# Layer 3 of a four-layer graph network: attention over 440 groups of 512 edges, rewritten with other operands, lead times and buffers

## The reference

```python
h = jnp.maximum(_layernorm(x, axis=-1), 0.0)
# _L3_gnn_ref(h, rel_embed_weight, W, heads=src, rels=edge_type_64, tails=dst)
e_h = entity_emb[heads]
e_t = entity_emb[tails]
e_r = rel_embed_weight[rels]
score = jnp.sum(e_t * jnp.tanh(e_h + e_r), axis=-1)
score_exp = jnp.exp(score - lax.stop_gradient(jnp.max(score)))
score_sum = jax.ops.segment_sum(score_exp, heads, num_segments=n_entities)
attn = score_exp / (score_sum[heads] + 1e-10)
agg = jax.ops.segment_sum(attn[:, None] * e_t, heads, num_segments=n_entities)
out = (entity_emb + agg) @ W.T
return jax.nn.leaky_relu(out, negative_slope=0.2)
```

## Time and profile before

| | us |
|---|---|
| median of 3 runs | 12000.16 |
| lowest, highest run | 11994.03, 12004.05 |
| profiled execution, its own time | 12014.41 |
| its span | 12012.6 |
| PE busy (share of the span) | 8140.2 (68%) |
| PEld busy | 6349.2 (53%) |
| DVE busy | 8287.7 (69%) |
| ACT busy | 4862.3 (40%) |
| POOL busy | 6896.0 (57%) |
| first record load of layer 3 | at 9149.8 |

### The profile page before, as it was taken

One profiled execution on the slowest core, in us unless ns is written; L12 is line 12 of the kernel. 1 busy time (PEld: TensorE's weight loads), 2 busy tenths in 40 slices (PEclk: granted clock), 3 DMA queues, 4 the chain that ended last, 5 costly groups with the idle time before them and its releaser, 6 DMA issues. The chain is left out here.

```text
span 12012.6 us, 257271 instructions
## 1 busy us (share of the span) xinstructions
PE 8140.2 (68%) x63022; PEld 6349.2 (53%) x63685; DVE 8287.7 (69%) x33874; ACT 4862.3 (40%) x9481; POOL 6896.0 (57%) x7087
## 2 busy tenths in 40 slices
PE   0222222255888888867766777777755999999996
PEld 0222222234566555556545666666653777777775
DVE  7444444426888888878526999999987666666664
ACT  3000000003777777722103555555542444444442
POOL 1777777722777777720004777777753666666662
PEclk9999999998888888889857999999987999999997
DMA  3333333330222222146301222222252333333345
GB/s 116 80 80 80 80 80 80 78 29 24 61 60 59 59 58 58 50 121 175 104 11 34 60 59 60 60 59 60 60 46 64 98 99 98 98 99 98 98 97 59
DMA packets 863125, 886.04 MB, mean 74 GB/s; under 512 B 466669, under 2 KB 636430, under 8 KB 862693
## 3 DMA queue, kind: packets, MB, share of 16 engines
q0 software_dynamic: 254464, 511.95, 18.7%
q1 hardware_dynamic: 608613, 373.57, 12.0%
HBM read 699.65 MB, written 155.84 MB: 71 GB/s over the span
## 5 line engine op out<-in xcount | busy, mean ns | idle before, releaser
L1291 POOL DMA_INDIRECT a_far<-node_table,a_rows x3552 | 3464.3, 975 | 3242.7 <-DMA a_rows<-edge_records 1256.1
L1069 POOL DMA_INDIRECT message_records<-f_msg,f_index x1760 | 1746.3, 992 | 924.2 <-issue 528.1
L897 POOL DMA_INDIRECT sum_far<-split_table,sum_rows x1760 | 1669.2, 948 | 669.4 <-issue 631.9
L982 PE MATMUL banks<-sum_far,sum_hot 128*128 128x128 bf16 x5280 | 635.5, 310 | 1711.8 <-DMA sum_far<-split_table,sum_rows 1604.8
L982 PEld LDWEIGHTS banks<-sum_far,sum_hot 128*128 128x128 bf16 x5280 | 528.2, 143 | 1819.0 <-issue 891.1
L964 ACT ACTIVATE acc<-sum_cur 128x128 f32 x880 | 272.2, 309 | 2752.8 <-DVE sum_cur L926 2415.6
L926 DVE SCALAR_TENSOR_TENSOR sum_cur<-sum_cur,gsame,banks 128x128 f32<-128x128 f32 x880 | 303.0, 344 | 1253.6 <-PE banks L982 1250.5
L1429 PE MATMUL banks<-ident,a_score 128*128 128x128 f32 x7072 | 997.1, 287 | 223.2 <-DVE a_score L1351 197.5
L1449 PE MATMUL banks<-a_far,a_prob 128*128 128x129 f32 x7056 | 1029.6, 291 | 0.0
L1429 PEld LDWEIGHTS banks<-ident,a_score 128*128 128x128 f32 x7072 | 994.5, 202 | 32.3
L1393 ACT ACTIVATE a_hot_t<-banks 128x512 bf16<-128x512 bf16 x888 | 521.4, 587 | 1038.6 <-PE banks L1438 749.9
(11 more groups left out here) (271 smaller groups left out, 19179.5 us busy)
## 6 DMA issues: line engine op xcount, KB each, us to landing
a_rows<-message_records SPq DMA_DIRECT2D x446, 264.0 KB
sum_rows<-message_records SPq DMA_DIRECT2D x441, 264.0 KB
acc<-a_cur SPq DMA_DIRECT2D x880, 65.0 KB
a_far<-node_table,a_rows POOLq DMA_INDIRECT x3552
sum_far<-split_table,sum_rows POOLq DMA_INDIRECT x1760
message_records<-f_msg,f_index POOLq DMA_INDIRECT x1760
f_attr<-edge_attributes SPq DMA_DIRECT2D x447, 40.0 KB
edge_attributes<-in_edge_attr SPq DMA_DIRECT2D x8, 1953.1 KB, 33.7
```

The lines of the kernel that those rows point to most:

```text
L897: pool.indirect_dma_start(far[:, u, q, :], None, k.table3[:, :], bass.IndirectOffsetOnAxis(ap=rows[:, u, q, C_SRC:C_SRC + 1].bitcast(I32), ...
L982: last = nc.tensor.matmul(k.psum[a % 2][:, 0:D], hot[:, u, q, :], rhs, start=q == 0 and part == 0, stop=q == KG - 1 and part == (2 if o == ...
L1069: pool.indirect_dma_start(k.mrec[:, :], bass.IndirectOffsetOnAxis(ap=index[:, u, q:q + 1], axis=0), msg[:, u, q, :], None, bounds_check=ED ...
L1291: pool.indirect_dma_start(far[:, u, q, 0:D], None, k.table[:, :], bass.IndirectOffsetOnAxis(ap=rows[:, u, q, other:other + 1].bitcast(I32) ...
```

## The change

Layer 3 no longer calls `attention(k, 1)` but a function of its own, `relation(k)`; layer 2 still uses `attention`. In `relation`:

- The record load takes only the last four words of each edge (512 pieces of 16 bytes a group) into eight buffers, with a lead of 10.
- `columns` (lead 7) makes `rel`, `kind` and `hide`. PE spreads the two as rows over all partitions (`spread_keys`, lead 6: eight bf16 matmuls of a broadcast column with the identity), ACT copies the 128x1024 result as bf16 (`take_keys`), and DVE compares each with the partition's number, which gives the one-hots with edges on the free axis at once (`one_hots`, lead 5: two instructions of 128x512). L1438, L1440, L1392, L1393 and the four-times-two comparisons go.
- The relation's first two parts lie on partitions 0 to 63 and 64 to 127 of one operand, so a block of 128 edges takes two matmuls for it instead of three (`near`, lead 4). The tanh is written back to PSUM, and the score reads it there (lead 3).
- One running maximum over all edges and windows takes the place of one per node. DVE reduces the scores of a partition to one (`peak`), PE spreads the 128 peaks (one f32 matmul), DVE takes their maximum. ACT takes the exponentials of the 128x4 scores only. DVE builds the weighted one-hots in f32 (`weigh`, lead 1: compare and multiply, four instructions of 128x128), with edges on partitions, as PE needs them for the sums. L1427, three of the four f32 matmuls of L1429, L1476, L1386, L1398 and L1359 go.
- The gather has a lead of 6 and eight buffers. `CREDIT` grows to 16 so that no count starts below zero; in layers 1 and 2 it only changes by how much counts are raised at the start.

```diff
--- before.py
+++ after.py
-CREDIT = 10
+CREDIT = 16
 ...
-        rel_f = sb(top, "rel_f", [NTYPE, D])
-        rel3 = sb(top, "rel3", [NTYPE, 3 * D], BF16)
+        rel_f = sb(top, "rel_f", [P, D])
+        rel2 = sb(top, "rel2", [P, 2 * D], BF16)
+        part_id, part_i = sb(top, "part_id", [P, 2]), sb(top, "part_i", [P, 1], I32)
 ...
-                split3(nc, lambda ins: link(dve, ins), rel3[:, 0:D], rel3[:, D:2 * D], rel3[:, 2 * D:3 * D],
-                       rel_f[:, :], relr)
+                split3(nc, lambda ins: link(dve, ins), rel_hi, rel_mid, rel_lo, rel_f[:, :], relr)
+                nc.vector.tensor_copy(rel2[0:NTYPE, 0:D], rel_hi[0:NTYPE, :])
+                nc.vector.tensor_copy(rel2[NTYPE:P, 0:D], rel_mid[NTYPE:P, :])
+                nc.vector.tensor_copy(rel2[0:NTYPE, D:2 * D], rel_lo[0:NTYPE, :])
+                nc.vector.tensor_copy(part_id[:, 0:1], part_i[:, :])
+                link(dve, nc.vector.tensor_scalar(part_i[:, :], part_i[:, :], NTYPE - 1, None, ALU.bitwise_and))
+                link(dve, nc.vector.tensor_copy(part_id[:, 1:2], part_i[:, :]))
 ...
-        attention(k, 1)
+        relation(k)
 ...
+def relation(k):
+    LOAD, COLS, KEYS, GATHER, HOT, NEAR, SCORE, MAX, WEIGH, ADD = 10, 7, 6, 6, 5, 4, 3, 2, 1, 0
+    S, H = 2 * U, 4
 ...
+                def load(g, a):
+                    wait(sp, now, scores, g, a, S)
+                    e0 = first_edge(sp, k, o, g + a)
+                    sp.dma_start(rows[:, a % S, :, :], k.mrec[bass.ds(e0, GE), M_SRC:MW].bitcast(I32).rearrange("(p q) c -> p q c", q=KG))\
+                        .then_inc(loads_in[a % S], 16)
 ...
+                skewed(sp, (LOAD, load), (ADD, keep), counts=now, turn=S)
 ...
+                def gather(g, a):
+                    u = a % S
+                    pool.wait_ge(loads_in[u], slot_count(now, g, a, 16, S, s_load[u]))
+                    wait(pool, now, summed, g, a, S)
+                    pool.sem_inc(k.begun, 1)
+                    for q in range(KG):
+                        pool.indirect_dma_start(
+                            far[:, u, q, 0:D], None, k.table[:, :],
+                            bass.IndirectOffsetOnAxis(ap=rows[:, u, q, M_DST - M_SRC:M_DST - M_SRC + 1], axis=0))\
+                            .then_inc(gathered[u], 16)
+                skewed(pool, (GATHER, gather), counts=now, turn=S)
 ...
+                def columns(g, a):
+                    u = a % S
+                    dve.wait_ge(loads_in[u], slot_count(now, g, a, 16, S, s_load[u]))
+                    nc.vector.tensor_scalar(rel[:, u, :], rows[:, u, :, 0], k.gbase[o][:, bass.ds(g + a, 1)], None, ALU.subtract)
+                    nc.vector.tensor_copy(kind[:, u, :], rows[:, u, :, M_TYPE - M_SRC]).then_inc(cols_ready, 1)
+                    wait(dve, now, cols_ready, g, a)
+                    nc.vector.tensor_scalar(hide[:, u, :], rel[:, u, :], float(P), -BIG, ALU.is_ge, ALU.mult)
+                def one_hots(g, a):
+                    h, b = a % H, a % 2
+                    wait(dve, now, keys_taken, g, a)
+                    wait(dve, now, near_ready, g, a, H)
+                    nc.vector.tensor_scalar(hot_t[:, h, :], keys[:, b, 0, :], k.part_id[:, 0:1], None, ALU.is_equal)
+                    nc.vector.tensor_scalar(kind_t[:, h, :], keys[:, b, 1, :], k.part_id[:, 1:2], None, ALU.is_equal)\
+                        .then_inc(onehotT_ready, 1)
+                def score_edges(g, a):
+                    u, b = a % S, a % 2
+                    dve.wait_ge(gathered[u], slot_count(now, g, a, 16 * KG, S))
+                    wait(dve, now, edge_term, g, a)
+                    wait(dve, now, scores, g, a, 1)
+                    for q in range(KG):
+                        last = nc.vector.scalar_tensor_tensor(
+                            work[:, q, :], near_ps[b][:, q * D:(q + 1) * D], 1.0, far[:, u, q, 0:D], ALU.mult, ALU.mult,
+                            accum_out=raw[:, q:q + 1])
+                    last.then_inc(edge_dot, 1)
+                    wait(dve, now, edge_dot, g, a)
+                    wait(dve, now, weighed, g, a, S)
+                    nc.vector.tensor_tensor(score[:, u, :], raw[:, :], hide[:, u, :], ALU.add).then_inc(masked, 1)
+                    wait(dve, now, masked, g, a)
+                    wait(dve, now, spread, g, a, S)
+                    nc.vector.tensor_reduce(peak[:, u:u + 1], score[:, u, :], AX, ALU.max).then_inc(scores, 1)
+                def running_max(g, a):
+                    u, f = a % S, bass.ds(g + a, 1)
+                    past = cur[:, (u - 1) % S, D + 1:D + 2]
+                    wait(dve, now, exp_in, g, a, 1)
+                    wait(dve, now, shrink, g, a, S)
+                    nc.vector.tensor_scalar(before[:, u:u + 1], past, k.gfresh[o][:, f], None, ALU.add)
+                    wait(dve, now, spread, g, a)
+                    nc.vector.tensor_reduce(gmax[:, :], peak_ps[a % 2][:, 0:P], AX, ALU.max).then_inc(group_max, 1)
+                    dve.wait_ge(kept, now(g, 16 * (a + 1), 16))
+                    wait(dve, now, group_max, g, a)
+                    nc.vector.scalar_tensor_tensor(cur[:, u, D + 1:D + 2], gmax[:, :], -1.0, past, ALU.mult, ALU.min)\
+                        .then_inc(exp_in, 1)
+                def weigh(g, a):
+                    u, b = a % S, a % 2
+                    wait(dve, now, weighed, g, a)
+                    wait(dve, now, summed, g, a, 2)
+                    for q in range(KG):
+                        last = nc.vector.tensor_scalar(share[:, b, q, :], k.iota_b[:, :], rel[:, u, q:q + 1],
+                                                       prob[:, u, q:q + 1], ALU.is_equal, ALU.mult)
+                    last.then_inc(prob_ready, 1)
+                def add(g, a):
+                    u, b = a % S, a % 2
+                    wait(dve, now, summed, g, a)
+                    wait(dve, now, shrink, g, a)
+                    wait(dve, now, added, g, a, 1)
+                    nc.vector.scalar_tensor_tensor(cur[:, u, 0:D + 1], cur[:, (u - 1) % S, 0:D + 1], factor[:, u:u + 1],
+                                                   sum_ps[b][:, 0:D + 1], ALU.mult, ALU.add).then_inc(added, 1)
+                skewed(dve, (HOT, one_hots), (ADD, add), (WEIGH, weigh), (SCORE, score_edges), (MAX, running_max), (COLS, columns),
+                       counts=now, turn=S)
+            @block.scalar
+            def _(act):
+                now = Counts(act)
+                start(act, keys_taken, edge_term, weighed, shrink)
+                def take_keys(g, a):
+                    wait(act, now, keys_spread, g, a)
+                    wait(act, now, onehotT_ready, g, a, 2)
+                    nc.scalar.activation(keys[:, a % 2, :, :], key_ps, ACT.Copy).then_inc(keys_taken, 1)
+                def terms(g, a):
+                    b = a % 2
+                    wait(act, now, near_ready, g, a)
+                    nc.scalar.activation(near_ps[b], near_ps[b], ACT.Tanh).then_inc(edge_term, 1)
+                def exps(g, a):
+                    u = a % S
+                    wait(act, now, exp_in, g, a)
+                    wait(act, now, prob_ready, g, a, S)
+                    nc.scalar.activation(prob[:, u, :], score[:, u, :], ACT.Exp, bias=cur[:, u, D + 1:D + 2]).then_inc(weighed, 1)
+                    wait(act, now, added, g, a, S)
+                    nc.scalar.activation(factor[:, u:u + 1], before[:, u:u + 1], ACT.Exp, scale=-1.0,
+                                         bias=cur[:, u, D + 1:D + 2]).then_inc(shrink, 1)
+                skewed(act, (KEYS, take_keys), (NEAR, terms), (MAX, exps), counts=now, turn=S)
+            @block.tensor
+            def _(pe):
+                now = Counts(pe)
+                start(pe, keys_spread, near_ready, spread, summed)
+                def spread_keys(g, a):
+                    u = a % S
+                    wait(pe, now, cols_ready, g, a)
+                    wait(pe, now, keys_taken, g, a, 1)
+                    for i, col in enumerate((rel, kind)):
+                        for q in range(KG):
+                            last = nc.tensor.matmul(key_ps[:, i, q * P:(q + 1) * P], top_half(col[:, u, q:q + 1]), k.ident_b[:, :],
+                                                    start=True, stop=True)
+                    last.then_inc(keys_spread, 1)
+                def near(g, a):
+                    h, b = a % H, a % 2
+                    w = window(pe, k, o, g + a)
+                    wait(pe, now, onehotT_ready, g, a)
+                    wait(pe, now, scores, g, a, 2)
+                    for q in range(KG):
+                        span = slice(q * P, (q + 1) * P)
+                        for part in range(3):
+                            nc.tensor.matmul(near_ps[b][:, span], hot_t[:, h, span], k.near[:, w, part * D:(part + 1) * D]
+                                             .rearrange("p a d -> p (a d)"), start=part == 0, stop=False)
```

(19 more changed lines are left out.)

69 lines of the change are left out of this document (63 added, 6 removed).

## The result

| | us |
|---|---|
| after, median of 4 runs | 11562.61 (11560.19 to 11566.87) |
| before, median of 4 runs | 11998.98 (11994.03 to 12004.05) |
| ratio | 0.9637, 95% interval 0.962 to 0.9653 |
| profiled execution after, and its span | 11562.07, 11560.3 |

The change makes the kernel 436 us faster. That is the predicted side and inside the range, 42 us above the forecast of 11521 and 3 us above the band of 11486 to 11560 that the prediction gave the forecast itself.

What follows compares the result with a forecast made beforehand. POOL's gathers replace PE as layer 3's limit: 1784 x 1.252 = 2234 us plus 35 for padding, 479 us less in all. The profiled 12014.4 becomes 11535, which lies 14 above the median: 11521, range 11480 to 11720.

Steps and rivals of the forecast that it cites:

- the band of 11486 to 11560: Whole kernel: span of the forecast itself, from the padding's bounds and a few us at the ends; chance 0.66.
- The bound moves from PE to POOL: Layer 3: POOL's four gathers a group, 1.252 us each, set the pace at 5.01 us instead of PE's 6.08.
- the keys: PE in layer 3: the eight matmuls spreading the keys take 0.8 us a group, between 0.76 and 1.44.
- The clock of 0.88: PE in layer 3: at layer 1's granted clock its 3.8 us a group become 4.3.
- The load of the window's number: PE's own queue in layer 3: costed at nothing behind 1.9 us of queued work, up to 1.0 us if late.
- the 0.7 that the prediction promised: Layer 3: DVE would wait some 0.7 us a group for gathers ahead of its products.
- The first rival: Layer 3: DVE or PE ends above POOL; 174 us more, 11695, span 11560 to 11920; chance 0.22.
- 46 ns for each piece: Layer 3's DMA: 1152 pieces at this price take 53 us of the 80 a group has, hidden.
- The rule on the shared port: A two-port tensor_scalar locks GpSimd out of writing descriptors; six such instructions a group would be felt on POOL.
- The rival that built on it: Layer 3: gathers wait for VectorE's comparisons and weighing, 1.3 us a group, 580 us more, 12101; chance 0.04.
- Its sign of being wrong by DMA: Layer 3: POOL's gathers waiting for record loads would show the prediction wrong.
- The padding's term: Layer 3's last 27 groups: 108 gathers at layer 0's 1.57 us each add 35 us, bounds nothing and 68.

Runs made afterwards that it cites:

- Run 3: The changed kernel with PE spreading the peaks four times instead of once a group in layer 3, three more f32 matmuls; 11585.75 us.
- run 1: The changed kernel with layer 3 issuing two of its four gathers a group, output not the reference's; 11437.25 us against 12029.83 for the kernel before.
- run 8: run 1 with 40 groups instead of 8 in a round of layer 3's loops; 11193.85 us against 12010.86 for the kernel before.
- Run 4: The kernel before with only layer 3's narrow record load, four words an edge; 12020.22 us against 12029.83 for the kernel before.
- Run 5: The changed kernel with the padding message records naming different target rows instead of one common row; 11516.44 us, ratio 0.9588.
- run 6: Run 5 with the edge records' padding, loaded by layers 0 to 2, also naming different source rows; 11451.91 us, ratio 0.9536.
- run 10: The changed kernel with 40 groups in a round of layer 3's loops, on a chip where the kernel before took 14715.03 us; 14586.38 us, ratio 0.9905.

## Why the prediction was right, and where it was off

- **The bound moves from PE to POOL**: right. 5.03 us a group against 5.01, gathers 1.25 us apart across groups, and 5.2 us of waiting for `summed` in 1700 us. Run 3 (more PE work, same pace) and run 1 (half the gathers, faster) show it from both sides.
- **PE**: it is hidden, as forecast; its 1472.2 us busy are 4.36 a group, where 4.3 were costed, but partly by luck. At the full clock a turn of PE takes 3.61 us (run 1, 10014.19 to 10017.80) for the 3.8 costed: the keys 0.45 instead of 0.8, the sums 0.99 instead of 0.88. The clock of 0.88 was taken over from layer 1's messages, and the 0.91 measured came from DVE's stall, which the prediction did not have. The load of the window's number was put at nothing; PEld stands some 0.48 us in front of the node rows in nearly every turn (147.1 us in 307 times), which stayed hidden too. Run 3's three more matmuls still found room.
- **DVE**: 4.3 predicted, and a turn that nothing disturbs lasts 4.24 (runs 1 and 8). Within it the weighings are 0.23 dearer (1.03 for 0.8), and products and masking what they were costed at. Missing from the sum was the stall at the end of a loop's round, 3.2 us in eight groups and 5.2 with PE's slower turns behind it: 4.24 + 5.2 / 8 = 4.89, and the next limit is at 4.885 (run 1) instead of 4.3. That is the step that failed. The profile before could not have priced it: in its layer 3, with as many groups in a round, DVE never stands longer than 1.6 us. It stayed hidden, but by 0.15 us and not by the 0.7 that the prediction promised as DVE's wait for gathers; in fact its products waited 47.9 us in the whole stage for them. The first rival was nearer than its chance of 0.22 made it look.
- **DMA**: 46 ns for each piece was wrong for pieces of 16 bytes. Run 4 shows 21 ns as the mean, the share fell from 0.36 to 0.30 although a group is shorter, where 0.5 to 0.65 was forecast. The term was hidden either way.
- **The rule on the shared port** (the Trainium skill, SBUF — State Buffer, "Who interferes with whom"): the trace still speaks against it for these instructions. With two comparisons of 128x512 and four weighings a group the gathers last 954 ns on average (1288.43 / 1351), where layer 0's last 948 (1471.87 / 1553); at most these 6 ns could be the port's. The rival that built on it, 12101 us, is out.
- **Where the 42 us lie.** Start: the first gather at 9146.2, not 9157, because the code before it ran shorter than in the profiled execution before (layer 2's first gather is at 6423.1 already, where it was at 6433.9): -11. Pace: 1672 gathers in 2104 us (to 11250.2) are 1.258 each, not 1.252, by the 6 ns that a gather lasts longer: +11. Padding: the last 112 gathers took 189 us, 1.69 each, where 1.57 was taken over 108 of them: 189 - 112 x 1.252 = 49 instead of 35, +14. End: 16 us from the last gather to the next stage instead of 2: +14. That is +28 against 11535, and the profiled execution was 11562 (+27). The remaining 14 are the offset from the profiled execution to the median: it was a property of that one execution before, and did not come back (11562.07 profiled, 11562.61 median).

Of the signs that the prediction named, POOL's busy share, the distance of the gathers and the 0.35 us of the comparisons came true. Three did not: PE is busy 87% and not 75% to 85%, DVE hardly waits for gathers, and the DMA share is 0.30. Its sign of being wrong by DMA, gathers that wait for record loads, is there in the padding only, 34.0 us.

The padding's term was taken from layer 0 rather than from layer 3's own 1.88: the truth lies between. Run 5 names its cause, one common row, which the prediction used and did not look into; run 6 shows that it is worth more than a quarter of what the change itself gives (121 of 436 us).

## What to carry to other kernels

When one engine is relieved, cost the others with everything that comes with them: here the 0.30 us in front of each gather, and the 3 us that DVE stands at the end of a loop's round, which short rounds pay often. Such a stand costs more than itself where another engine then idles and its clock falls. When the next limits lie within a few per cent of each other, halve the new limit's work once on the chip: it shows how far away the next one is. Let the padding of an indirect load point to many rows, never to one.

## What the runs showed of the hardware

- At the end of a loop's round DVE stands about 3.1 us with the bodies of `relation`, whether a round has 8 groups or 40 (runs 1 and 8). With the bodies of layer 3 before, also 8 groups a round, it never stands longer than 1.6 us; the cause is open.
- At the stand of some 2 us that PE makes behind it, PE's granted clock fell to the lower level, about once a round, and the four f32 sums lasted 2.09 us instead of 1.16 (run 1). In layer 3 before, where PE was busy 99%, the granted clock was 1.00.
- Gathers of 128 rows start 1.25 us apart (0.94 busy, 0.30 between), in layer 0 as in layer 3 beside DVE's comparisons, and 1.25 to 1.30 inside a group on the chip of run 10. When all pieces read one row the DMA engines go from 0.21 to 0.91 busy, and with the waits for late records and sums a gather takes 1.69 us on average (run 5 and the profile after).
- 1152 pieces, 512 of them of 16 bytes, take less DMA engine time than 768 with records of 2112 bytes: 24 against 35 us a group (run 4).
- One chip ran the same code of layers 0 to 2 a quarter slower (11473 against 9146 us to the first gather of layer 3, run 10), and on it and on a second one the kernel before took 14715 and 14461 us. Engines stood and the clock was lower, and of its 3.6% the change kept about 1% there, together with the long loop: a gain measured on one chip need not be another's.
